# A two-layer decoder on one core: short operations of the second self attention moved to GpSimd and ScalarE, another start for VectorE, and a new order of the work

## What is computed

```python
def _layernorm(x, axis=-1, eps=1e-05):
    m = jnp.mean(x, axis=axis, keepdims=True)
    v = jnp.var(x, axis=axis, keepdims=True)
    return (x - m) / jnp.sqrt(v + eps)
...
    x = x + _L0_attn_ref(_layernorm(x, axis=-1), L0_attn_Wq, L0_attn_Wk, L0_attn_Wv, ...)
    x = x + _L0_xattn_ref(_layernorm(x, axis=-1), ctx_1024, ctx_1024, L0_xattn_Wq, ...)
    x = x + _L0_ffn_ref(_layernorm(x, axis=-1), L0_ffn_w1, L0_ffn_conv_w, L0_ffn_conv_b, L0_ffn_w2)
    x = x + _L1_attn_ref(_layernorm(x, axis=-1), L1_attn_Wq, L1_attn_Wk, L1_attn_Wv, L1_attn_Wp, L1_attn_bp)
    x = x + _L1_xattn_ref(_layernorm(x, axis=-1), ctx_1024, ctx_1024, L1_xattn_Wq, ...)
    x = x + _L1_ffn_ref(_layernorm(x, axis=-1), L1_ffn_gate_w, L1_ffn_gate_b, L1_ffn_w1, ...)
    return x
```

```python
attn = jax.nn.softmax(jnp.einsum('bhqd,bhkd->bhqk', q, k) * scale, axis=-1)
attn = attn + rel_bias
out = jnp.einsum('bhqk,bhkd->bhqd', attn, v)
...
scores = jnp.where(causal, -jnp.inf, scores)
scores = (scores + _alibi_bias(t, scores.dtype)) / jnp.sqrt(jnp.asarray(DQ, scores.dtype))
w = jax.nn.softmax(scores, axis=-1)
ctx = jnp.einsum('bhqk,bhkd->bqhd', w, v).reshape(b, t, D_OUT)
return ctx @ Wp + bp
```

## Time and profile before

| | |
|---|---|
| median of 3 runs | 604.96 us (604.09 to 607.64) |
| the profiled execution, its own time | 606.53 us |
| its span in the trace | 604.6 us |
| TensorE's mean granted clock | 0.95 |
| lane B's first FFN product issued / x updated by it | 309.8 us / 335.0 us |

### The profile page before, as it was taken

One profiled execution on the slowest core, in us unless ns is written; L12 is line 12 of the kernel. 1 busy time (PEld: TensorE's weight loads), 2 busy tenths in 40 slices (PEclk: granted clock), 3 DMA queues, 4 the chain that ended last, 5 costly groups with the idle time before them and its releaser, 6 DMA issues.

```text
span 604.6 us, 13037 instructions
## 1 busy us (share of the span) xinstructions
PE 522.7 (86%) x4832; PEld 323.9 (54%) x4842; DVE 427.1 (71%) x1261; ACT 330.7 (55%) x819; POOL 191.4 (32%) x288
## 2 busy tenths in 40 slices
PE   1888789999999889777877798899878998999996
PEld 1433345444455656555544455676546886655554
DVE  5796665545567565788688788755567746699896
ACT  1663445565678677559257354466546743453441
POOL 7860000042237444423430310000123321354674
PEclk9975789999999999898897899999989999999997
DMA  8700000000030000000084342100000000303001
GB/s 291 285 3 3 2 2 4 1 2 1 1 140 1 1 2 2 1 2 1 1 277 128 106 129 87 36 3 4 1 1 3 3 3 1 125 16 141 0 2 35
DMA packets 25890, 27.93 MB, mean 46 GB/s; under 512 B 18250, under 2 KB 22867, under 8 KB 24931
## 3 DMA queue, kind: packets, MB, share of 16 engines
q1 hardware_dynamic: 25826, 27.10, 13.5%
HBM read 22.14 MB, written 4.75 MB: 44 GB/s over the span
## 4 chain that ended last, share of the span: by engine, by line
PE 64%; DVE 19%; ACT 5%; issue 5%; POOL 3%; DMA 2%; SPq 1%; POOLq 0%; DVEq 0%; ACTq 0%; another core or an unknown queue 0%
PE A_banks L312 4%; PE B_banks L312 4%; PE A_banks L2098 3%; PE B_banks L2098 3%; PE A_banks L1020 2%; PE A_banks L1007 2%; DVE A_l0a_nmax L340 2%; PE B_banks L1007 2%; PE B_banks L1823 2%; PE B_banks L1020 2%; PE B_banks L248 1%; PE B_banks L975 1%; PE A_banks L975 1%; PE B_banks L962 1%; PE B_banks L960 1%
## 5 line engine op out<-in xcount | busy, mean ns | idle before, releaser
L825 POOL TENSOR_TENSOR B_l0x_prob<-B_l0x_prob,B_l0x_inverted_sums 128x256 f32<-128x256 f32 (+1 forms) x32 | 26.0, 834 | 43.6 <-DVE B_l0x_inverted_sums L940 43.6
L825 POOL TENSOR_TENSOR A_l0x_prob<-A_l0x_prob,A_l0x_inverted_sums 128x256 f32<-128x256 f32 (+1 forms) x32 | 25.9, 829 | 39.3 <-DVE A_l0x_inverted_sums L940 39.2
L379 ACT ACTIVATE A_l0a_expT<-A_banks 128x512 f32<-128x512 f32 x32 | 18.6, 608 | 29.5 <-PE A_banks L327 29.5
L2098 PE MATMUL A_banks<-A_moe_xT,w_moe_rows 128*128 128x512 f32 x72 | 34.5, 597 | 0.1
L2098 PE MATMUL B_banks<-B_moe_xT,w_moe_rows 128*128 128x512 f32 x72 | 34.0, 595 | 0.0
L340 DVE TENSOR_REDUCE A_l0a_nmax<-A_banks 128x2 f32<-128x512 f32 x32 | 21.8, 689 | 14.6 <-PE A_banks L248 14.1
L842 ACT ACTIVATE A_l0x_prob<-A_l0x_prob,A_l0x_nmax 128x128 f32<-128x128 f32 x64 | 28.2, 447 | 2.5 <-DVE A_l0x_nmax L922 2.5
L842 ACT ACTIVATE B_l0x_prob<-B_l0x_prob,B_l0x_nmax 128x128 f32<-128x128 f32 x64 | 28.2, 446 | 0.9 <-DVE B_l0x_nmax L922 0.9
L340 DVE TENSOR_REDUCE B_l0a_nmax<-B_banks 128x2 f32<-128x512 f32 x32 | 21.8, 687 | 9.0 <-PE B_banks L248 8.6
L160 POOL TENSOR_TENSOR A_l0a_rstd<-A_l0a_ve,w_const_rows 128x4 f32<-128x4 f32 x2 | 2.0, 1012 | 79.9 <-DVE A_l0a_ve L156 79.9
L379 ACT ACTIVATE A_l1a_expT<-A_banks 128x384 f32<-128x384 f32 x32 | 15.3, 494 | 20.1 <-PE A_banks L292 20.1
(11 more groups left out here) (603 smaller groups left out, 1582.0 us busy)
## 6 DMA issues: line engine op xcount, KB each, us to landing
w_toeplitz_rows<-in_toeplitz_rows SPq DMA_DIRECT2D x1, 3072.0 KB, 13.6
w_moe_rows<-in_moe_rows SPq DMA_DIRECT2D x1, 2304.0 KB, 9.8
w_l1x_rows<-in_l1x_rows SPq DMA_DIRECT2D x1, 2048.0 KB, 8.7
A_l1x_values<-A_l1a_v_tokens SPq DMA_DIRECT2D x4, 512.0 KB, 3.6
A_l1x_v_groups<-A_l1x_values SPq DMA_DIRECT2D x16, 128.0 KB, 3.3
B_l1x_values<-B_l1a_v_tokens SPq DMA_DIRECT2D x4, 512.0 KB, 3.0
B_l1x_v_groups<-B_l1x_values SPq DMA_DIRECT2D x16, 128.0 KB, 3.2
w_l0x_vo_rows<-in_l0x_vo_rows SPq DMA_DIRECT2D x1, 1024.0 KB, 13.8
```

What stands on the lines that cost most here:

```text
L379: act.activation(self.expT[:, u % self.ring, :], self.exp_bank(u)[:, 0:self.W], ACT.Exp, scale=self.scale).then_inc(self.s_p.sem, 1)
L825: ins = pool.tensor_tensor(pair, pair, bcast(rz[:, g % 2, i, :], 2, n), ALU.mult)
L2098: pe.matmul(hidden_bank(k)[:, :], w["moe_w3" if which else "moe_w1"][:, ORDER[i], part, :], xT[:], start=True, stop=True).then_inc(s_h.sem, 1)
```

## The change

**The first self attention.** For lane A only (`early`), the fill of `vals` goes from GpSimd to VectorE, as VectorE's first instruction. In both lanes the column of ones stands behind the power of the variance, and further `yield`s cut the first turn into smaller ones.

**The second self attention.** The fills of kT and `vals` go from VectorE to GpSimd, in front of its power of the variance; since they are the first turn, GpSimd's own wait for x comes after both, with the turn behind it. The column of ones goes to GpSimd too. `mid` and `lo` of the split go to GpSimd, the four copies of `qT` to ScalarE; the copy of `kT` stays on VectorE with a semaphore of its own. ScalarE's copy of the values waits for the rest (`s_rest`) and no longer for the whole split.

**The order.** `TURNS` is new for every engine, from the first turn to the last. Lines behind the changed ones have moved: those of the first stage's products, L960 of l0x and so on, stand 7 lines lower in the second and third stage and about 10 lower behind the fourth.

```diff
@@ -431,6 +431,7 @@
     s_stk = st.sem("k_stack_ready", TT)
     s_init = st.sem("buffers_set", 3)
     s_stT = st.sem("stack_transposed", STEPS)
+    early = lane.name == "A"
     by_scalar = [n % 4 == 3 or n >= 4 * SB for n in range(STEPS)]
     s_qkT = st.sem("qkT_by_vector", STEPS - sum(by_scalar))
     s_qkA = st.sem("qkT_by_scalar", sum(by_scalar))
@@ -479,15 +480,18 @@
 
     def gpsimd(pool):
         yield 0.0
-        pool.memset(vals[:], 0.0).then_inc(s_init.sem, 1)
+        if not early:
+            pool.memset(vals[:], 0.0).then_inc(s_init.sem, 1)
+        yield 0.5
         pool.memset(stack[:, :, 0, :, 6 * HD:SW], 0.0)
         pool.memset(stack[:, :, 1, :, 6 * HD + 3:SW], 0.0)
         pool.memset(stack[:, :, 1, :, 6 * HD:6 * HD + 3], 1.0).then_inc(s_init.sem, 1)
-        pool.wait_ge(*s_init(2))
-        pool.memset(vals[:, :, :, 16 + HD:16 + HD + 1], 1.0).then_inc(s_init.sem, 1)
         yield 2.0
         w.loaded(pool, "const")
         norm.gpsimd_rstd(pool)
+        yield 2.0
+        pool.wait_ge(*s_init(2))
+        pool.memset(vals[:, :, :, 16 + HD:16 + HD + 1], 1.0).then_inc(s_init.sem, 1)
         yield 2.1
         w.ready(pool, lane, "x")
         for t in range(TT):
@@ -561,6 +565,9 @@
     def vector(dve):
         link = Chain(dve, lane)
         yield 0.0
+        if early:
+            dve.memset(vals[:], 0.0).then_inc(s_init.sem, 1)
+        yield 0.5
         w.ready(dve, lane, "x")
         yield from norm.vector_stats(dve, link, x)
         yield
@@ -1315,10 +1322,11 @@
     s_vs = st.sem("ctx_values_stored", 16 * TT)
     s_rb = st.sem("row_bias_ready", 2)
     s_xn, s_xTp, s_xT = st.sem("xn_ready", TT), st.sem("x_transposed", 1), st.sem("xT_ready", 1)
-    s_qkv, s_split, s_v = st.sem("qkv_ready", TT), st.sem("parts_ready", TT), st.sem("values_ready", TT)
+    s_qkv, s_v = st.sem("qkv_ready", TT), st.sem("values_ready", TT)
+    s_rest, s_mid, s_split = st.sem("rest_ready", TT), st.sem("middle_parts_ready", TT), st.sem("parts_ready", TT)
     s_stq, s_stk = st.sem("q_stack_ready", TT), st.sem("k_stack_ready", TT)
     s_init, s_kz = st.sem("buffers_set", 2), st.sem("keys_and_values_zeroed", 2)
-    s_stT, s_qkT = st.sem("stack_transposed", 5), st.sem("qkT_ready", 5)
+    s_stT, s_qT, s_kT = st.sem("stack_transposed", 5), st.sem("qT_ready", 4), st.sem("kT_ready", 1)
     s_ob, s_fin = st.sem("o_transposed", GROUPS), st.sem("o_finished", GROUPS)
     s_xb, s_yTp, s_yT = st.sem("x_bias_ready", 1), st.sem("y_transposed", 1), st.sem("yT_ready", 1)
     s_wp, s_x = st.sem("product_ready", TT), st.sem("x_updated", TT)
@@ -1366,11 +1374,16 @@
             a.sync_shift(sp, k)
 
     def gpsimd(pool):
+        yield 0.5
+        pool.memset(kT[:], 0.0).then_inc(s_kz.sem, 1)
+        pool.memset(vals[:], 0.0).then_inc(s_kz.sem, 1)
         yield 1.5
         w.loaded(pool, "l1a")
         norm.gpsimd_rstd(pool)
         yield 1.6
         yield 2.0
+        pool.wait_ge(*s_kz(2))
+        pool.memset(vals[:, :, :, DV:DV + 1], 1.0).then_inc(s_init.sem, 1)
         parts = w["alibi_q"]
         pool.tensor_tensor(row_bias[:], parts[:, :, :, 3], parts[:, :, :, 4], ALU.add).then_inc(s_rb.sem, 1)
         pool.memset(stack[:, :, :, 6 * DQ + 6:SW], 0.0)
@@ -1384,7 +1397,14 @@
         ins.then_inc(s_init.sem, 1)
         pool.tensor_tensor(xb[:], x[:], w["l1a_bp"][:].unsqueeze(1).broadcast_to([P, TT, D]), ALU.add).then_inc(s_xb.sem, 1)
         for t in range(TT):
-            yield 9.0 + 3.5 * t
+            yield 8.5 + 3.5 * t
+            pool.wait_ge(*s_rest(t + 1))
+            mid, lo, rest = sp_[:, t % 2, 1, :], sp_[:, t % 2, 2, :], sr[:, t % 2, :]
+            pool.tensor_copy(mid, rest).then_inc(s_mid.sem, 1)
+            yield
+            pool.wait_ge(*s_mid(t + 1))
+            pool.tensor_tensor(lo, rest, mid, ALU.subtract).then_inc(s_split.sem, 1)
+            yield
             pool.wait_ge(*s_split(t + 1))
             for part, i, n in split_columns(Q_PARTS):
                 out = stack[:, t, 0:H, i * DQ:(i + n) * DQ].rearrange("p h (n d) -> p h n d", n=n)
@@ -1402,8 +1422,10 @@
             ins.then_inc(s_key.sem, 1)
 
         def values(t):
+            act.wait_ge(*s_rest(t + 1))
+            act.activation(vals[:, t, :, 0:DV], bank[2 + t % 2][:, NQK:W].rearrange("p (h d) -> p h d", h=HK), ACT.Copy).then_inc(s_v.sem, 1)
+            yield 9.5 + 3.5 * t
             act.wait_ge(*s_split(t + 1))
-            act.activation(vals[:, t, :, 0:DV], bank[2 + t % 2][:, NQK:W].rearrange("p (h d) -> p h d", h=HK), ACT.Copy).then_inc(s_v.sem, 1)
             for part, i, n in split_columns(K_PARTS):
                 out = stack[:, t, H:H + HK, i * DQ:(i + n) * DQ].rearrange("p h (n d) -> p h n d", n=n)
                 src = sp_[:, t % 2, part, NQ:NQK].rearrange("p (h d) -> p h d", h=HK).unsqueeze(2).broadcast_to([P, HK, n, DQ])
@@ -1425,9 +1447,13 @@
                 yield 9.0 + 3.5 * t
                 if t == 0:
                     act.wait_ge(*s_init(2))
-                values(t)
+                yield from values(t)
 
         yield from interleaved([all_keys(), all_values()])
+        for g in range(4):
+            yield 22.0 + g
+            act.wait_ge(*s_stT(g + 1))
+            act.activation(qT[:, g, :], stack_bank(g).bitcast(BF16), ACT.Copy).then_inc(s_qT.sem, 1)
         for n in range(U + 8):
             yield LOOP + STEP * n
             if n < U:
@@ -1462,17 +1488,11 @@
                 dve.wait_ge(*s_stq(t - 1))
                 dve.wait_ge(*s_stk(t - 1))
             qk = bank[2 + t % 2][:, 0:NQK]
-            hi, mid, lo = (sp_[:, t % 2, i, :] for i in range(3))
+            hi = sp_[:, t % 2, 0, :]
             link.add(dve.tensor_copy(hi, qk))
             yield due
             link.wait()
-            link.add(dve.tensor_tensor(sr[:, t % 2, :], qk, hi, ALU.subtract))
-            yield due
-            link.wait()
-            link.add(dve.tensor_copy(mid, sr[:, t % 2, :]))
-            yield due
-            link.wait()
-            dve.tensor_tensor(lo, sr[:, t % 2, :], mid, ALU.subtract).then_inc(s_split.sem, 1)
+            dve.tensor_tensor(sr[:, t % 2, :], qk, hi, ALU.subtract).then_inc(s_rest.sem, 1)
 
         def all_values():
             for m in range(0, JOBS, 2):
@@ -1482,9 +1502,6 @@
                 values(m)
 
         def all_splits():
-            yield 3.0
-            dve.wait_ge(*s_kz(2))
-            dve.memset(vals[:, :, :, DV:DV + 1], 1.0).then_inc(s_init.sem, 1)
             for t in range(TT):
                 yield 8.0 + 3.5 * t
                 yield from split(t, 8.0 + 3.5 * t)
@@ -1493,22 +1510,14 @@
         yield from norm.vector_stats(dve, link, x)
         yield
         norm.vector_apply(dve, xn, x, s_xn)
-        dve.memset(kT[:], 0.0).then_inc(s_kz.sem, 1)
-        dve.memset(vals[:], 0.0).then_inc(s_kz.sem, 1)
         yield from interleaved([all_values(), all_splits()])
-        for g in range(5):
-            yield 22.0 + g
-            if g == 4:
-                dve.wait_ge(*s_kz(2))
-            dve.wait_ge(*s_stT(g + 1))
-            src = stack_bank(g).bitcast(BF16)
-            if g < 4:
-                ins = dve.tensor_copy(qT[:, g, :], src)
-            else:
-                for j in range(HK):
-                    r = slice(SW * j, SW * (j + 1))
-                    ins = dve.tensor_copy(kT[r, j, :], src[r, :])
-            ins.then_inc(s_qkT.sem, 1)
+        yield 26.0
+        dve.wait_ge(*s_kz(2))
+        dve.wait_ge(*s_stT(5))
+        for j in range(HK):
+            r = slice(SW * j, SW * (j + 1))
+            ins = dve.tensor_copy(kT[r, j, :], stack_bank(4).bitcast(BF16)[r, :])
+        ins.then_inc(s_kT.sem, 1)
         for u in range(a.first):
             yield SCORES + 3.0 + 0.75 * u
             if u == a.JOBS:
@@ -1593,7 +1602,7 @@
                 pe.wait_ge(*s_init(2))
                 pe.wait_ge(*s_v(TT))
             if g >= 2:
-                pe.wait_ge(*s_qkT(g - 1))
+                pe.wait_ge(*s_qT(g - 1))
             for t in range(TT):
                 if t:
                     yield
@@ -1605,7 +1614,8 @@
         for u in range(a.first):
             yield SCORES + 3.0 + 0.75 * u - 0.4
             if u == 0:
-                pe.wait_ge(*s_qkT(5))
+                pe.wait_ge(*s_qT(4))
+                pe.wait_ge(*s_kT(1))
                 wait_job(pe, JOBS - 2)
                 wait_job(pe, JOBS - 1)
             if u == a.JOBS:
@@ -2399,37 +2409,36 @@
 TURNS = {
     "tensor":
...
     "vector":
-        "A3 W1 A1 B3 A3 B1 A3 B2 A1 B2 A4 B2 A3 B2 A2 B3 A1 B1 W1 A5 B1 A1 B1 A1 B1 A2 B1 A5 B2 A1 B1 A1 B1 A3 B1 A1 B1 A2 B1 A2 B1 A1 B2 A2 B1 A1 B1 A2 B1 A1 "
...
+        "A5 W1 B4 A2 B1 A4 B2 A1 B2 A4 B1 A1 B1 A2 B5 A2 B1 A1 B1 W1 B1 A5 B6 A1 B2 A1 B1 A1 B1 A1 B2 A5 B2 A2 B1 A3 B1 A2 B1 A2 B2 A1 B1 A1 B2 A2 B2 A1 B1 A1 "
...
     "sync":
-        "W1 A1 W1 B1 W11 A1 B1 A1 B1 A2 B2 L1 A1 L1 A7 B3 A1 B2 A1 B4 A1 B1 A1 B2 A2 B2 A1 B1",
```

(1 more changed line is left out.)

4 lines of the change are left out of this document (2 added, 2 removed), and 45 rows, old and new, of the table TURNS.

## The result

The changed kernel takes 585.59 us (median of 4 runs, 577.98 to 586.47) against 604.93 us: a ratio of 0.965, 95% interval 0.958 to 0.973. It is faster by 19.3 us. The profiled execution has 586.47 us and a span of 584.7 us, 19.9 less than before.

What follows compares the result with a forecast made beforehand. TensorE was taken as the main bound (busy 522.7 of 604.6 us), VectorE in the FFNs. Gains 3.2 + 0 + 3.7 + 1.0 = 7.9 us off 606.53 gave 598.6, or 597 us as median; range 588 to 607.

Steps and rivals of the forecast that it cites:

- The beginning: Kernel start: lane A's normalisation starts at 9.1 instead of 12.3 us, behind lane B's fills; gain 3.2 us.
- The rival in which VectorE gets in first: Kernel start: normalisation starts at 6.8 us, and half of the clock's 10 us comes; 590.5 us, chance 0.10.
- The second self attention: Operations moved off VectorE there gain 1.9 us, less 1.3 for later powers and 0.6 for hold-ups: 0.
- The added wait: Second self attention: GpSimd's fills make its power of the variance start 0.65 us later per lane, 1.3 us in all.
- The order: New instruction order: lane A's FFN behind most of lane B's cross attention, lane B's FFN right after; gain 3.7 us.
- So 82 take 17.3: Lane B's 82 extra instructions ahead of lane A's FFN move its start from 256.7 to 274.0 us.
- Then comes lane A's FFN, at the pace of lane B's: Lane A's FFN in the new order takes 24.5 us, ending at 298.5 us; slow end 35.4 us.
- 7.6 us that the new order leaves for later: TensorE's work on lane A's next stage before lane B's FFN, from 302.2 to 309.8 us, is postponed.
- both lanes' FFNs meet on VectorE: Lane A's FFN shares VectorE with lane B's work and takes 35.4 us or more; up to 611 us, chance 0.17.
- The clock: From 44 to 80 us, packing lane B's scores between lane A's raises TensorE's clock; gain 1.0 us, ends 0 and 10.
- what is gained goes on waits: GpSimd's fills hold up VectorE for 4.7 us and the order gives nothing; 605 us, chance 0.15.
- two table loads fewer: ScalarE has 6 function table loads instead of 8, 1.28 us each, with no exponentials between the two FFNs.

Runs made afterwards that it cites:

- e1: Kernel before with the new first-stage code and, up to lane A's first split, the new order of VectorE, GpSimd and SyncE: 600.78 us, ratio 0.994.
- e4: Kernel before with new beginning and new order until lane B leaves its FFN, then old order and old second self attention code: 588.33 us, ratio 0.977.
- e7: Kernel before with new beginning and new order until lane B leaves the first self attention, old order and code after: 598.79 us, ratio 0.988.
- e8: Kernel before with new beginning and new order until lane B leaves its cross attention and starts its FFN, old after: 596.24 us, ratio 0.986.
- e2: Kernel before with new order and new second self attention code only from where lane B starts that stage: 600.90 us, ratio 0.995.
- e6: Kernel before with new beginning and new order until lane A leaves the first self attention, old order and code after: 597.98 us, ratio 0.990.
- e3: Changed kernel in its full new order, but with the old code of the second self attention: 587.99 us, ratio 0.975.

## Why the prediction was wrong in size

**The beginning** (forecast 3.2 us, measured 3.4): right, and so was its reason, that the normalisation would wait for lane B's fills. The first transpose is at 9.08 us, forecast 9.5. The rival in which VectorE gets in first, with the transpose at 7.2 us, comes out in none of the twelve profiles; what I had no case for is VectorE coming in behind the first of the fills, as it does in four of them (8.0 us). e1's own profile is one of the other eight.

**The second self attention** (forecast 0, measured about 2 for the code, with intervals that overlap, and 3.0 with its order): within reach of the upper end of 1.9. The added wait cost 0.4 us in one lane and nothing in the other where I had 0.65 in each, and the fills cost VectorE's other operations 0.5 and 0.4 us in lane A and 0.4 in lane B, where I took 0.6 for both lanes. Which of the moved operations brings the 2 us was not tried.

**The order** (forecast 3.7): this step failed, and with it the total. With the clock I had 4.7 us; measured are 10.3 (e4's 13.7 less e1's 3.4, by the ratios), before the second self attention's code and order. The step had three parts.
- "So 82 take 17.3": they cost 8.7. Lane A's first FFN product is at 251.3 us in e7 and at 260.0 in e8, which has them in front; the clocks of the two profiles are alike (0.88 and 0.87 up to 44 us, 0.74 and 0.77 from there to 80). Against e1 (252.3) it is 7.7, and the three profiles of the changed kernel (258.5 to 262.7) put it at 6 to 10. The price per instruction, from the busy time of such rows, was fair: lane B's products in front of that place keep TensorE busy for 120.0 us in e8 and 105.5 in e7, 14.4 more. What I had wrong is that all of it would come on top. TensorE's whole busy time rises by 11.7 us, as lane A's products there, the same in number, take 2.4 less, and its idle time falls by 3.0. Why lane A's products are shorter is open.
- "Then comes lane A's FFN, at the pace of lane B's", 24.5 us: measured 26.4 (262.7 to 289.1). Right, and the two bounds of 24.5 and 35.4 were well drawn.
- "7.6 us that the new order leaves for later": I took them out in front and let them be paid in full behind. They were not. Lane B's FFN took 29.2 us with this work inside (288.9 to 318.1) instead of 24.5 + 7.6 = 32.1, and all that lies behind it got shorter too. The 7.6 us were also too small a measure of what stood in the way: with lane B's cross attention gone from in front, 18.7 us still pass between the two FFNs in e8. Without them lane A's FFN is 2.4 us longer in e4 and lane B's 7.2, so 9.1 us are won.

Put together at the end of lane B's FFN: before 334.3 us, by my sum 334.3 - 3.2 - 3.7 - 1.0 = 326.4, measured 318.1 (8.3 sooner). From there to the end: 270.3 before and by my sum, 266.6 measured (3.7). The two make the 12 us between 598.6 and 586.5.

The larger point is one that I had turned the wrong way: I made a rival of "both lanes' FFNs meet on VectorE" and gave it the slow end, because VectorE is busy for 80.0 of 97 us there. It is the head of lane B's FFN beside lane A's, and lane A's next work beside lane B's, that brought 5 to 10 us. A share of 82% was no sign that VectorE was full. From lane A's first FFN product to lane B's last it was busy for 65.5 of 77.6 us before (84%) and is busy for 49.6 of 55.2 us now (90%). That rival is refuted: lane A's FFN takes 26.4 us and not 35.4.

**The clock** (forecast 1.0, ends 0 and 10): too small in the stretch that I looked at, and blind to the one ahead of it. Take busy time times the missing share of the clock, by windows. From 44 to 80 us it is 10.0 us before (9.5 and 12.9 in e1 and e2, which have the old order there) and 6.4 to 7.8 in the fourteen profiles with the new order up to there: 1.7 us or more are saved, 2.2 to 3.6 against the kernel before. The step from e1 to e6, which gives both lanes the new order up to the end of lane A's first self attention, is of the same size, 2.8 us; that the clock is all of it was not tried. From 20 to 44 us it is 2.5 us before and anything from 0 to 5.3 with the new order, because the clock falls near 32 us in some executions and near 42 in others. The first profile of the changed kernel has 13.1 us in both stretches together, the second 8.3, the kernel before 12.5, so one profile does not tell.

The rival "what is gained goes on waits" (605 us) is refuted by the total, and by e4 and e3. The forecast that ScalarE's list has two table loads fewer came out: 6 instead of 8, 1.28 us each.

## What to carry to other kernels

With two chains of short dependent steps on the same engines, let the head of one run beside the body of the other rather than behind it, even where one engine looks 80% busy: before calling it full, look at what ended its idle times. Work that an order postpones is not paid at its busy time; it is paid at what of it finds no gap, so count the gaps of the place where it goes. And put GpSimd's long fills where VectorE has no copies, casts or tensor-scalar operations to issue: ahead of a power of the variance, not behind it.

## What was unexpected of the hardware

- A VectorE operation that waits for one of GpSimd's back-to-back fills does not surely get in behind it. In eight profiles of twelve three fills passed ahead of one tile of the normalisation, which took 2,111 ns instead of 343; in four only the first did (1,050 ns). Both came in executions of one kernel.
- A fill of 3,072 float32 columns on VectorE and one on GpSimd ran at the same time at 2.62 and 2.66 us, so this pair does not hold each other up.
- The moment at which TensorE's granted clock falls to its 1.2 GHz level differs between executions of one kernel, near 32 or near 42 us. At lane A's first exponentials this makes 3.5 us (47.0 against 43.5).
